# A new launch order in a gated cross-attention and FFN kernel: setup loads, Wq split by output columns, and re-planned instruction orders

## The reference

```python
q = layernorm(x) @ Wq.T + bq;  k = ctx @ Wk.T + bk;  v = ctx @ Wv.T + bv
scores = einsum('bgrqd,bgkd->bgrqk', q, k) / sqrt(16)
scores = where(causal_mask | padding_mask, -inf, scores)
out = softmax(scores) @ v
x = x + tanh(g_xattn) * (out @ Wo.T + bo)
h = layernorm(x)
fuse = silu((h @ fp8(gate_w)) * gate_scale) * ((h @ fp8(up_w)) * up_scale)
x = x + tanh(g_ffn) * ((fuse @ fp8(down_w)) * down_scale)
```

## Time and profile before

| | |
|---|---|
| three runs | 613.05 us (609.72 to 614.7) |
| the profiled execution | 617.89 us |
| its span, first to last instruction | 616.1 us |
| outside the span | 1.8 us |
| mean granted TensorE clock | 0.961 |
| PE busy in the span | 563.3 us (91%) |
| DVE, ACT, POOL busy | 485.9, 363.7 and 255.8 us |

### The profile page before, as it was taken

One profiled execution on the slowest core, in us unless ns is written; L12 is line 12 of the kernel. 1 busy time (PEld: TensorE's weight loads), 2 busy tenths in 40 slices (PEclk: granted clock), 3 DMA queues, 4 the chain that ended last, 5 costly groups with the idle time before them and its releaser, 6 DMA issues.

```text
span 616.1 us, 14167 instructions
## 1 busy us (share of the span) xinstructions
PE 563.3 (91%) x5056; PEld 348.4 (57%) x5056; DVE 485.9 (79%) x1505; ACT 363.7 (59%) x668; POOL 255.8 (42%) x339
## 2 busy tenths in 40 slices
PE   0846888799999999999999999999998999799997
PEld 0633343357754775467745765476645764376683
DVE  2377768999899889988999999988998898744321
ACT  3533675787754765556665576576644764475261
POOL 4043041123552078424464166306711464248274
PEclk9956999699999999999999999999997999799999
DMA  8662465571222033211322412112203000101000
GB/s 299 221 210 85 106 200 113 121 267 37 80 60 73 14 83 111 58 50 40 102 83 70 112 37 81 44 31 66 73 3 95 2 28 29 53 3 53 1 36 34
DMA packets 57158, 50.30 MB, mean 82 GB/s; under 512 B 8000, under 2 KB 46976, under 8 KB 57088
## 3 DMA queue, kind: packets, MB, share of 16 engines
q1 hardware_dynamic: 55600, 48.79, 26.9%
q10 hardware_dynamic: 1488, 0.61, 0.4%
HBM read 35.21 MB, written 9.44 MB: 72 GB/s over the span
## 4 chain that ended last, share of the span: by engine, by line
PE 73%; DVE 13%; issue 8%; POOL 2%; ACT 2%; DMA 1%; POOLq 0%; SPq 0%; DVEq 0%
PE work L982 25%; PE work L993 12%; PE av L890 8%; PE work L921 7%; PE work L960 5%; DVE junk L741 5%; PE sc L862 5%; PE sc L880 4%; DVE ws L750 2%; PE work L931 2%; DMA cin<-in_ctx_t 1%; PE work L907 1%; PE work L941 1%; PE sc L876 1%; PE work L969 1%
## 5 line engine op out<-in xcount | busy, mean ns | idle before, releaser
L741 DVE CUSTOM_DVE_ANT_0 junk<-sc,mq 128x256 bf16<-128x256 f32 x496 | 180.0, 418 | 26.5 <-PE sc L862 26.0
L750 DVE SCALAR_TENSOR_TENSOR ws<-sc,padc,mask_k 128x1024 f32<-128x1024 f32 x112 | 143.3, 1279 | 19.4 <-PE sc L880 18.0
L614 ACT ACTIVATE ws<-ws 128x1024 f32<-128x1024 f32 x112 | 116.8, 1053 | 19.7 <-DVE ws L750 19.4
L538 POOL TENSOR_TENSOR ff<-ga,up 128x256 f32<-128x256 f32 x96 | 69.3, 729 | 120.7 <-DVE ga L826 117.0
L982 PE MATMUL work<-h_h,wg 128*128 128x256 f16 x384 | 90.4, 276 | 0.0
L982 PE MATMUL work<-h_l,wg 128*128 128x256 f16 x384 | 89.8, 274 | 0.0
L982 PE MATMUL work<-h_h,wu 128*128 128x256 f16 x384 | 89.4, 273 | 0.0
L982 PE MATMUL work<-h_l,wu 128*128 128x256 f16 x384 | 89.3, 273 | 0.0
L674 ACT ACTIVATE up<-work,fuse_s 128x256 f32<-128x256 f32 x96 | 45.2, 471 | 55.5 <-PE work L982 55.5
L993 PE MATMUL work<-wd,f_h 128*128 128x512 fp8e4 x192 | 73.0, 380 | 0.1
L993 PE MATMUL work<-wd,f_l 128*128 128x512 fp8e4 x192 | 72.8, 379 | 0.0
(11 more groups left out here) (116 smaller groups left out, 1013.6 us busy)
## 6 DMA issues: line engine op xcount, KB each, us to landing
qs<-q_scratch SPq DMA_DIRECT2D x96, 64.0 KB, 2.4
xin<-in_x SPq DMA_DIRECT2D x8, 512.0 KB, 4.6
cin<-in_ctx_t SPq DMA_DIRECT2D x8, 512.0 KB, 4.5
xb<-in_x SPq DMA_DIRECT2D x8, 512.0 KB, 4.7
att_u<-un SPq DMA_DIRECT2D x128, 32.0 KB, 2.0
out_x<-yt SPq DMA_DIRECT2D x16, 256.0 KB, 2.2
ks<-k_scratch SPq DMA_DIRECT2D x48, 64.0 KB, 2.4
q_scratch<-qh SPq DMA_DIRECT2D x16, 128.0 KB, 2.5
```

Of the source, the lines that this page charges most:

```text
L538: pool.tensor_tensor(ff[:, n % RING, :], ga[:, n % RING, :], up[:, n % RING, :], ALU.mult).then_inc(ff_done, 1)
L614: act.activation(ws[:, unit, :, :], ws[:, unit, :, :], ACT.Exp, scale=1.0 / SSC).then_inc(exp_done, 1)
L741: last = dve.tensor_tensor_reduce((junk, junk_1)[maxima_banks(n, b)][:, j, :], sc[maxima_banks(n, b)][:, place(j)], mq[b % 2][:, t, :], 1. ...
L750: dve.scalar_tensor_tensor(out=ws[:, n % 4, :, :], in0=sc[1][:, :].rearrange("p (j l) -> p j l", j=HPG), scalar=padc[b % 2][:, kt:kt + 1], ...
```

## The change

It does four things together.

- The setup DMAs are issued in another order. x of batch 0 is loaded in two halves, one by SP and one by ACT; Wq in two halves by output columns, with semaphores of their own; the padding rows come ahead of Wo; Wk comes behind the small tables on ACT.
- `Wq0` and `Wq1` are now the halves by output columns, so the first `q` needs only `Wq0`. Every setup piece has its own pair of semaphores, and can stand anywhere in the lists, under its own name.
- `get_k` of batch 0 is issued by ACT in place of SP. The bf16 copies of the mask and of the identity on POOL are a piece of their own, `mask_b`. PE's wait for the identity moves from its start to the first `xT`.
- All five lists are written anew. They hold the same pieces apart from those two. PE makes the same matmuls as before.

```diff
-def order(words, setup=(), by_pe=0):
+def order(words, by_pe=0, k_by_act=0):
...
-            if name == "setup":
-                pieces.append((name, setup[k], 0))
+            if name in SETUP:
+                pieces.append(("setup", SETUP.index(name), 0))
...
 ACT_ORDER = order("""
-    setup cT*2 setup*2 norm1 k xT*2 q setup*2 slab*2 gates setup q norm1 xT*2 cT q cT slab mrow norm1 q k exp*3 slab
+    slab Wk norm1 Wq0 xT*2 cT Wq1 cT q Wo0 k Wv gates q get_k norm1 xT*2 cT*2 slab norm1 slab q*2 Wo1 mrow k exp*2
...
 PE_ORDER = order("""
-    k xT*2 q*2 v xT*2 maxima*3 q maxima*6 mrow q maxima k maxima scores maxima scores xT maxima scores weighted
+    xT*2 q k q v xT*2 maxima*2 q maxima*2 q maxima k maxima*4 mrow v xT maxima*2 scores maxima scores maxima scores
...
 SP_ORDER = order("""
-    load_c slab*2 load_x put_k put_q get_k get_q slab load_x put_q slab get_q slab put_q rows get_q put_k load_c
+    slab load_x slab put_q put_k load_c get_q load_x slab load_xb put_q get_q put_q rows put_k get_q load_c slab*2
...
+            if name[1] == "q":
+                i = wq_columns(int(name[2]))
+                return st_q[:, :, i], wq_h[:, :, i], wq_l[:, :, i], SWQK, ld_wq[int(name[2])]
...
+        def get_k(eng, b):
+            eng.wait_ge(k_out, 32 * (b + 1))
+            past(eng, t_ready, 16 * (b - 1))
+            if b < 2:
+                eng.wait_ge(sm_rows, 2)
+            for hf in range(2):
+                for s in range(3):
+                    src = k_dram[(0, 0, 1)[s]].rearrange("(g d) n -> d g n", d=HD)
+                    eng.dma_start(ks[b % 2][64 * hf + HD * s:64 * hf + HD * (s + 1), :, :], src).then_inc(ks_in, 16)
...
-            sp.dma_start(xin[:, :, :], x_v[0]).then_inc(ld_x, 16)
-            sp.dma_start(st_q[:, :, :], Wq_t.rearrange("(t p) i -> p t i", p=P)).then_inc(ld_wq, 16)
+            wq_v = Wq_t.rearrange("(t p) i -> p t i", p=P)
+            sp.dma_start(xin[:, 0, :], x_v[0][:, 0, :]).then_inc(ld_x, 16)
+            sp.dma_start(st_q[:, :, wq_columns(0)], wq_v[:, :, wq_columns(0)]).then_inc(ld_wq[0], 16)
             sp.dma_start(cin[:, :, :], c_v[0]).then_inc(ld_c, 16)
-            sp.dma_start(st_o[:, :, :], Wo_t.rearrange("(t p) i -> p t i", p=P)).then_inc(ld_wo, 16)
+            sp.dma_start(st_q[:, :, wq_columns(1)], wq_v[:, :, wq_columns(1)]).then_inc(ld_wq[1], 16)
...
-                act.activation(w_h, stage, ACT.Copy, scale=scale).then_inc(set_high, 1)
+                act.activation(w_h, stage, ACT.Copy, scale=scale).then_inc(set_high[SETUP[n]], 1)
+                if name == "get_k":
+                    get_k(act, b)
...
-                    if b == 0 and n == 0:
-                        pe.wait_ge(set_free, SETUP.index("Wq1") + 1)
+                    if b == 0:
+                        pe.wait_ge(set_free[f"Wq{n}"], 1)
```

More of the change, by code:

```diff
@@ L56 @@
           "slab": 12, "put_q": 2, "get_q": 2, "rows": 2, "gather": 2, "store": 2, "add_y": 2}
-def order(words, setup=(), by_pe=0):
-    pieces, seen = [], {"scores": PIECES["scores"] * by_pe, "load_x": 1, "load_c": 1}
+def order(words, by_pe=0, k_by_act=0):
+    pieces, seen = [], {"scores": PIECES["scores"] * by_pe, "load_x": 1, "load_c": 1, "get_k": k_by_act}
     for word in words.split():
@@ new lines @@
+    xT*2 q k q v xT*2 maxima*2 q maxima*2 q maxima k maxima*4 mrow v xT maxima*2 scores maxima scores maxima scores
+    xT maxima scores maxima weighted scores maxima weighted scores mrow maxima scores maxima weighted scores maxima
+    q maxima scores q maxima scores weighted maxima scores weighted maxima scores*2 maxima weighted scores maxima
+    mrow k maxima scores weighted maxima scores maxima weighted scores maxima scores maxima scores v maxima weighted
+    scores spread scores xT spread xT maxima weighted scores out scores maxima mrow out q scores weighted maxima
@@ new lines @@
+    scores maxima weighted x2T*2 maxima scores q maxima scores weighted gu maxima scores gu*2 scores maxima k gu
+    weighted maxima scores gu mrow gu scores maxima gu weighted scores maxima gu scores gu maxima scores gu weighted
+    maxima scores v gu scores maxima weighted gu down_a maxima scores down_a spread maxima scores weighted spread
+    down_b xT maxima scores xT down_b maxima scores mrow out maxima out weighted maxima scores q scores weighted x2T
+    maxima scores x2T q scores maxima weighted gu*2 maxima scores gu maxima gu scores maxima weighted gu*2 maxima
@@ new lines @@
+    scores mrow gu*2 k scores maxima weighted gu scores maxima gu weighted scores maxima gu scores v gu scores
+    weighted down_a scores maxima down_a spread scores maxima down_b spread maxima weighted xT scores maxima down_b
+    mrow xT maxima scores out*2 scores weighted maxima q maxima weighted scores x2T maxima x2T q scores weighted
+    maxima gu scores gu maxima scores gu*2 maxima scores gu weighted maxima scores gu mrow maxima gu*2 weighted
+    scores maxima gu k scores gu scores weighted maxima scores gu maxima weighted scores v gu maxima scores down_a
@@ new lines @@
+    spread down_a maxima scores spread down_b xT maxima scores weighted xT maxima down_b mrow maxima scores out*2
+    weighted scores maxima q maxima weighted x2T*2 maxima scores q maxima gu scores gu scores maxima weighted gu
+    maxima scores k gu maxima scores weighted gu mrow maxima scores gu*2 scores maxima weighted gu*2 scores maxima v
+    weighted scores gu scores maxima gu scores gu maxima scores weighted down_a maxima down_a spread scores maxima
+    down_b spread weighted maxima scores down_b mrow maxima scores out maxima out weighted xT scores maxima xT
@@ new lines @@
+    weighted scores k maxima x2T*2 q*2 maxima scores gu*2 maxima scores weighted gu maxima scores gu maxima weighted
+    scores gu mrow maxima scores gu weighted scores maxima gu*2 scores maxima gu weighted scores maxima gu*2 maxima
+    scores down_a gu maxima scores weighted down_a scores maxima spread down_b maxima scores weighted spread down_b
+    maxima scores mrow out scores out weighted maxima scores weighted v scores maxima x2T*2 maxima weighted scores
+    gu maxima gu scores maxima gu scores gu maxima scores gu weighted maxima gu mrow scores maxima gu*2 maxima
@@ L182 @@
+    load_xb rows load_c get_q put_q den gather put_k store get_k rows store load_x put_q load_c get_q load_xb gather
+    rows den put_q store get_q put_k gather get_k rows get_q put_k rows gather put_q load_xb den store get_q gather
+    store get_k rows load_xb gather put_q get_q rows store den store gather rows load_xb store gather den store
+    gather store*4
+""", k_by_act=1)
 IN_BANKS = ("xT", "q", "k", "v", "spread", "out", "x2T", "gu")
@@ L327, in xattn_ffn @@
         ld_x, ld_c, ld_xb = sem("ld_x"), sem("ld_c"), sem("ld_xb")
-        set_high, set_free = sem("set_high"), sem("set_free")
+        set_high, set_free = [{name: sem(f"{part}_{name}") for name in SETUP} for part in ("high", "set")]
         sm_rows, rows_f, masks_f = sem("sm_rows"), sem("rows_f"), sem("masks_f")
@@ L901, in _ @@
                 if name == "xT":
+                    if n == 0 and b == 0:
+                        pe.wait_ge(ld_ident, 16)
                     if n == 0:
```

219 lines of the change are left out of this document (95 added, 124 removed).

## The result

The changed kernel takes 619.96 us in the median of five runs (618.01 to 624.88), the kernel before 612.28 us beside it (609.72 to 614.7). The ratio is 1.0146, with a 95% interval of 1.0111 to 1.0181: the change makes the kernel slower, by 7.7 us. That is inside the range given (608 to 622), but 4.6 us above the forecast of 615.4, where rival 1 stood (619.5).

What follows compares the result with a forecast made beforehand. PE was taken as the bound, busy 563.3 of 616.1 us, idling mostly in the first 60 us. Terms +5.7, -2.0, +0.5, -0.5, -1.4 gave +2.3 on the 613.05 median: 615.4 us, range 608 to 622.

Steps and rivals of the forecast that it cites:

- rival 1: Batch 0's scores: head delay kept in full, lower PE clock adds +4 at first exps; +6.5, 619.5 us; 0.25 with other slow ends.
- Slab first on ACT: Head of ACT's list: slab lands at 18.7, ahead of Wk and `norm1`, so `norm1` ends 5.7 us late.
- To the first `q`: From `norm1`'s end to PE's first `q`: 3.6 us, so the first `q` starts at 25.8, +5.6 us.
- To the first maxima: ACT's and DVE's chains meet within 0.2 us; first maxima at 44.3, +3.7 us, ends +2.5 and +6.
- To the first exp: Maxima pieces between `q` and `k`, then `mrow` at 59.1; first exp at 68.1, +4.2 us, ends +3 and +6.6.
- The exps and behind them: Batch 0's sixteen exps give back 0.5, +3.7 at the last; behind, the delay shrinks to +2.3 or so.
- Later lists: From about 140 us on, PE is full and its order nearly the same: 0, ends -4 and +4.
- rival 2: Two later windows with PE holes: new lists close one and half the other, 9 us won; 606.5 us; chance 0.15.
- Sum: Whole kernel: +5.7 at `norm1`, -2.0, +0.5, -0.5 and -1.4 after it, giving +2.3 us, 615.4 us.
- Rival 3: Head of ACT: slab does not hold it, `norm1` starts 3 to 4 us ahead of 14.90; 609 us; chance 0.05.

Runs made afterwards that it cites:

- after_again: The changed kernel, unaltered, run once more for a second profile; 620.19 us.
- before_slab_first: The kernel before, with one slab put at the head of ACT's list and its load ahead of the context's on SP; 623.6 us, ratio 1.0178.
- wv_early: The changed kernel with the low part of Wv right behind `k` on DVE; 620.85 us, 1.0139 of the kernel before.
- the second pair: Second profiles of both kernels, unaltered: the kernel before at 613.35 us and the changed kernel at 620.19 us.
- warm_scores: The changed kernel with unused matmuls added, eight ahead of each of seven maxima pieces, sixteen ahead of the first scores; 621.49 us, ratio 1.016.
- slab_late: The changed kernel with the first slab moved behind the first `q` on ACT; 611.12 us, 0.999 of the kernel before.
- slab_late_get_k: The changed kernel with ACT's first slab behind the first `q` and SP's batch 2 `get_k` ahead of two slab loads; 609.39 us (0.9956), again 608.32 us (0.9935).

## Why the prediction was right in kind and 4.6 us too low

- *Slab first on ACT.* Right in its mechanism, and the deciding step, shown both ways: taken out of the changed kernel it gives back 8.8 us, put into the kernel before it costs 11.8. `norm1` ended 6.7 us late where I had 5.7. ACT starts the slab at 19.73 (20.41 in after_again), where I had a landing at 18.7 with ends of 17.8 and 19.5, so it lies just beyond the late end. That came from two errors against each other: the issue at 9.79 instead of 12.2, since fourteen setup issues took SP 8.9 us where thirteen had taken 10.9, and the landing 9.9 us behind it instead of 6.5. The earlier issue did not bring it in earlier: before_slab_first issued it at 11.86 and had it at 19.83, with the same setup weights on their way. The Trainium skill, DMA: Bandwidth & Descriptors, "Anatomy of one DMA", whose 2.0 us and bytes over 436 GB/s are for one DMA issued by GpSimd, would put it at an estimated 13.6 (9.79 and 3.8). For this load, issued by SP behind fourteen others, the trace has it 6 us later.
- *To the first `q`.* 26.73 against 25.8: the step is right (3.6 us from `norm1`'s end, as forecast), its start is the slab's.
- *To the first maxima.* This term was mis-sized: +3.7 forecast, +5.7 in the first pair of profiles and +6.9 in the second. I had the two chains through ACT and DVE meet at 41.0, and priced the issues of `ks` on ACT, but not their landing: issued to 39.8, they are there at 45.5, and the maxima at 46.3. A landing of 5.8 us in the median and 6.15 of the last, with a context block and the loads of `qs` issued just ahead, against 2.5 before, is the missing part. The wait that I did see, `v` behind `wv_l`, is real (4.13 us) and costs nothing, as wv_early shows.
- *To the first exp.* `nm` at 61.1 and first exp at 69.34, against 68.1: +5.4 and, in the second pair, +7.6, where I had +4.2. The later start was carried on.
- *The exps and behind them.* This is the step that failed. I had the delay shrink, to 3.7 at the last exp and 2.3 behind. It grew: in the two pairs +7.3 and +11.4 at the last exp, +11.9 and +11.6 at the first `gu`. Two things stood there in its place. First the clock: PE was granted 0.50 from 60 to 75 us, the two mask matmuls of the first scores took 1.04 us where they take 0.59 in warm_scores, and over the first four intervals of the exps the delay grew by 2.0 and 3.7 us. I had left that to rival 1 and taken the second `mrow` for the gate of the ninth exp; the chain shows no wait for it. Second, between the last exp and the first `gu` the old lists take 39.4 to 39.5 us and the changed kernel 44.1 in one profile, with its wait of 3.56 us for `ks`, and 39.6 in the other, with 0.27. That a busy DVE would give part of a late start back (it is busy for 19.67 of 20 us) has no support either: before_slab_first has 9.4 to 10.8 us at the first maxima and 8.2 to 10.9 at the first `gu`, and slab_late keeps nearly all of its 10. Its lead over the kernel before goes in the same two places: 4.7 us at the first maxima, 6.5 at the first exp, 4.3 at the ninth, 3.7 at the last, 0.8 at the first `gu` (3.3, 3.9, 1.7, 1.1 and -2.0 in the second pair). The loads of `ks` in the wrong place are about the last 3 of these (slab_late waits 2.71 us for them, and slab_late_get_k leads by 1.4 to 4.5 at the first `gu`).
- *Later lists.* I put them at 0, with ends of -4 and +4. They are -4.9 us, by comparison of profiles and not by an experiment on them: 467.8 to 469.7 us behind the first `gu` in eleven profiles with the new lists, 472.8 to 474.7 in three with the old. That is rival 2's mechanism, at half of its price, and in one of the two windows that it named (520 to 540 us); the other, 100 to 120, lies in the head and did not pay.
- *Sum.* About +11.8 ahead of the first `gu` and -4.9 behind make +6.9 us by spans; the medians say +7.7. The forecast had +2.3 and 0. So the head was too low by 9.5 us and the rest too high by 4.9. That the time fell into the range is in part luck: the head's +11.8 alone would have made 624.9 us, outside it.
- *Rival 1* has its mechanism in the profile: the clock of 0.50, +2.0 and +3.7 us over four intervals where it said +4, and the ninth exp at +6.7 and +10.8 where it said +6 to +8. Its 619.5 us are right partly by luck, since it had neither the wait for `ks` nor the -4.9 us behind. What the clock alone costs stays open: warm_scores paid for it with as much PE time ahead of the first scores.
- *Rival 3* lacked its condition, the slab in place by 10. What it priced is what slab_late does: `norm1` at 10.55, 4.35 ahead of before where it said 3 to 4, and 611.1 us, not 609. Of that lead nothing is left in the median.

What stays open: why PE's matmuls become fast 3 us earlier in one execution of the kernel before than in the other, and why the head of the changed kernel differs by 3 us at the first `gu` between two executions, which is as much as several of these edits are worth. And the 0.5% of slab_late_get_k is less than its spans would give (604.7 and 605.2 against 611.5 and 616.1): the profiled executions of before were above its median, those of this version below.

## What to carry to other kernels

In a kernel whose later part runs full, find the event from which all the rest takes a fixed time (here the first `gu`, 468 or 473 us from the end), and price each edit by what it does to the date of that event; do not count on a busy engine in between to give a delay at the head back (of 9.4 to 10.8 us, 8.2 to 10.9 arrived here). A piece that waits for a load at the head of an in-order engine costs the landing time of that load, and an earlier issue need not bring the load in earlier when much is queued ahead of it (issued at 9.79 and 11.86, it was there at 19.73 and 19.83). And the longest wait is not the last one: behind a wait of 4.1 us stood one of 0.75 for small loads, and taking the first away gained nothing. Ask for each load of a critical chain what bulk is queued ahead of it.
